# Cross-attention scores with two heads on two row halves of the array, in a six-block Perceiver kernel

## The reference

```python
qh = (q @ Wq + bq).reshape(B, LQ, 16, 16)      # LQ = 256, B = 4
kh = (k @ Wk + bk).reshape(B, 4096, 16, 16)    # k = v = ctx_512
vh = (v @ Wv + bv).reshape(B, 4096, 16, 16)
attn = softmax(einsum('bhqd,bhkd->bhqk', qh, kh) / 4)
out = einsum('bhqk,bhkd->bhqd', attn, vh) @ Wo + bo
```

## Time and profile before

| what | us |
|---|---|
| median of 3 runs | 1431.14 |
| lowest and highest | 1427.41, 1432.78 |
| span of the profiled execution | 1429.1 |
| TensorE busy in it | 1375.6 |
| VectorE busy | 1055.1 |
| ScalarE busy | 922.1 |
| GpSimd busy | 287.6 |

### The profile page before, as it was taken

The page is one execution under the profiler, slowest core; times in us unless marked ns, Lnnn a source line. Parts: engine busy times, 40 slices in busy tenths (PEclk is TensorE's granted clock), DMA queues, the critical chain, the costliest instruction groups (busy, mean ns, idle before and its releaser), DMA issues.

```text
span 1429.1 us, 28070 instructions
## 1 busy us (share of the span) xinstructions
PE 1375.6 (96%) x11138; PEld 846.7 (59%) x11138; DVE 1055.1 (74%) x2114; ACT 922.1 (65%) x1899; POOL 287.6 (20%) x321
## 2 busy tenths in 40 slices
PE   7799999999999999999999999999999999989998
PEld 5355555555555545555554556556557999856666
DVE  4787777787777778777778888835876778767757
ACT  5366777767777767777767666672796664448731
POOL 3354222222222222122213100000003100001210
PEclk9899999999999999999999999999999999999999
DMA  6966555346554545655454743002402320347000
GB/s 184 163 145 143 119 118 111 77 102 130 116 127 92 102 84 125 128 115 113 81 97 101 184 73 61 2 1 60 119 18 65 112 67 1 91 112 155 2 1 30
DMA packets 95587, 133.19 MB, mean 93 GB/s; under 512 B 8864, under 2 KB 70944, under 8 KB 89504
## 3 DMA queue, kind: packets, MB, share of 16 engines
q1 hardware_dynamic: 95456, 131.40, 42.3%
HBM read 94.15 MB, written 37.22 MB: 92 GB/s over the span
## 4 chain that ended last, share of the span: by engine, by line
PE 79%; ACT 8%; DVE 8%; DMA 2%; issue 2%; SPq 1%; POOL 0%; DVEq 0%; ACTq 0%
PE psum L559 16%; PE psum L540 13%; PE psum L524 13%; ACT probs L783 4%; PE psum L2132 4%; PE psum L587 3%; PE psum L2106 3%; DVE peaks L685 3%; PE psum L626 3%; PE psum L1226 2%; PE psum L2851 2%; PE psum L1623 1%; PE psum L275 1%; PE psum L2861 1%; PE psum L2814 1%
## 5 line engine op out<-in xcount | busy, mean ns | idle before, releaser
L685 DVE TENSOR_REDUCE peaks<-psum 128x1 f32<-128x512 f32 x1024 | 643.3, 684 | 197.0 <-PE psum L524 196.4
L783 ACT ACTIVATE probs<-psum 128x512 f32<-128x512 f32 x1024 | 529.0, 615 | 83.3 <-PE psum L540 79.4
L524 PE MATMUL psum<-keysT,queriesT 96*128 96x512 bf16 x1024 | 390.1, 384 | 13.2 <-DMA keysT<-key_parts 7.9
L540 PE MATMUL psum<-queriesT,keysT 98*128 98x256 bf16 x2048 | 392.4, 274 | 6.1 <-ACT queriesT L846 2.4
L540 PEld LDWEIGHTS psum<-queriesT,keysT 98*128 98x128 bf16 x2048 | 176.3, 99 | 191.7 <-ACT probs L783 72.1
L559 PE MATMUL psum<-probs,values 128*17 128x256 f32 x4096 | 245.9, 380 | 0.0
L559 PEld LDWEIGHTS psum<-probs,values 128*17 128x17 f32 x4096 | 107.2, 97 | 102.6 <-issue 27.1
L524 PEld LDWEIGHTS psum<-keysT,queriesT 96*128 96x128 bf16 x1024 | 98.6, 96 | 90.9 <-issue 56.1
L918 POOL CAST key_parts<-key_f 128x512 bf16<-128x512 f32 x57 | 34.8, 611 | 518.0 <-ACT key_f L816 511.0
L816 ACT ACTIVATE key_f<-psum,bk 128x512 f32<-128x512 f32 x59 | 40.5, 687 | 120.7 <-PE psum L587 120.6
L587 PE MATMUL psum<-ctxT,wk 128*128 128x512 f32 x128 | 69.5, 625 | 2.4 <-DVE probs L728 0.9
(11 more groups left out here) (315 smaller groups left out, 1662.5 us busy)
## 6 DMA issues: line engine op xcount, KB each, us to landing
keysT<-key_parts SPq DMA_DIRECT2D x31, 768.0 KB, 7.7
key_parts<-key_parts SPq DMA_DIRECT2D x90, 256.0 KB
keysT<-key_parts SPq DMA_DIRECT2D x31, 512.0 KB, 10.1
ctx_nat<-in_ctx_dram SPq DMA_DIRECT2D x32, 256.0 KB, 3.0
keysT<-key_parts SPq DMA_DIRECT2D x31, 256.0 KB, 11.6
ctx_in<-in_ctx_dram SPq DMA_DIRECT2D x24, 256.0 KB, 5.9
ctx_turned<-ctxT SPq DMA_DIRECT2D x24, 256.0 KB, 4.4
ctx_T<-ctx_turned SPq DMA_DIRECT2D x12, 512.0 KB, 3.8
```

What stands on the lines that cost most here:

```text
L524: e.matmul(ps, self.queriesT[0:ROWS, u % 2, g * GH + j, t * P:(t + 1) * P], self.keysT[0:ROWS, i % RING, j, c * BANK:(c + 1) * BANK], star ...
L540: made = e.matmul(ps[:, j * S:(j + 1) * S], self.keysT[0:AUG, i % RING, j, kt * P:(kt + 1) * P], self.queriesT[0:AUG, u % 2, g * GH + j, : ...
L685: e.tensor_reduce(self.peaks[:, i % 2, pair, c:c + 1], k.ps(("max", n)), AX.X, ALU.max).then_inc(*self.peaked.up(n))
L783: e.activation(self.probs[:, t % RINGP, e2 * GH * S:(e2 + 1) * GH * S], k.ps(("scores", t, e2)), ACT.Exp).then_inc(*self.exped.up((t, e2)))
```

## The change

Head j now has partitions 64 j to 64 j + 63. keysT and queriesT get two planes: MAIN with four of the six part products (64 rows of each head) and REST with the other two and the two maximum rows (34 rows). A score is the sum of two matmuls, MAIN and REST. The maximum uses MAIN alone, 64 rows where it had 96. In a slot the PE issues eight score matmuls of 256 columns, in the order e2, plane, head; then both maxima (one of each head, one after the other), then the weighing, then jobs. A score bank now holds both e2 of one head, so both banks of a slot are signalled by the slot's last two matmuls. Fill keys, turn ctx, turn shift, normalize and make values of later batches move to the next slot with t % 4 == 1 (beside). The result of turn shift is kept by two ACT instructions for one; reading keys and query rows takes four DMAs for three, writing queries five for three. The stream jobs keep their slots.

```diff
+        def beside(slot, job, *numbers):
+            at(slot + (1 - slot) % BLOCK, job, *numbers)
...
-                slot = UNIT * u - 101 + 8 * c
+                slot = UNIT * u - 105 + 8 * c
...
-                    at(slot, "turn ctx", b, c)
+                    beside(slot, "turn ctx", b, c)
...
-                at(slot + 2, "fill keys", u, c)
+                beside(slot + 6, "fill keys", u, c)
...
-            at(SLOTS * i - 2, "turn shift", i)
+            beside(SLOTS * i - 3, "turn shift", i)
...
-                at(SLOTS * i + SLOTS + 4, "normalize", i)
+                beside(SLOTS * i + SLOTS + 4, "normalize", i)
...
-                at(SLOTS * NG * b - 97 + 6 * p, "make values", b, p)
+                beside(SLOTS * NG * b - 97 + 6 * p, "make values", b, p)
...
-            e.matmul(ps, self.queriesT[0:ROWS, u % 2, g * GH + j, t * P:(t + 1) * P],
-                     self.keysT[0:ROWS, i % RING, j, c * BANK:(c + 1) * BANK],
-                     start=True, stop=True).then_inc(*self.max_made.up(n))
+            e.matmul(ps, self.queriesT[own, MAIN, u % 2, g, qt * P:(qt + 1) * P],
+                     self.keysT[own, MAIN, i % RING, c * BANK:(c + 1) * BANK],
+                     start=True, stop=True).then_inc(*self.max_made[j].up(n))
...
-            for e2 in range(2):
-                if 0 <= t < TOTAL:
-                    kt, n = 2 * p + e2, (2 * t + e2) % HALVES
-                    ps = banks.use(n, w, ("scores", t, e2), (self.exped, (t, e2)))
-                    for j in range(GH):
-                        made = e.matmul(ps[:, j * S:(j + 1) * S], self.keysT[0:AUG, i % RING, j, kt * P:(kt + 1) * P],
-                                        self.queriesT[0:AUG, u % 2, g * GH + j, :], start=True, stop=True)
-                    made.then_inc(*self.scored.up((t, e2)))
-                if maxima and not e2:
-                    find_max(maxima[0], t)
+                ps = {}
+                for e2 in range(2):
+                    kt = 2 * p + e2
+                    for plane, rows in ((MAIN, HALF), (REST, TALL)):
+                        for j in range(GH):
+                            if j not in ps:
+                                ps[j] = banks.use(SCORES[(2 * t + j) % len(SCORES)], w, ("scores", t, j), (self.exped, (t, j)))
+                            own = slice(j * HALF, j * HALF + rows)
+                            made = e.matmul(ps[j][:, e2 * S:(e2 + 1) * S], self.keysT[own, plane, i % RING, kt * P:(kt + 1) * P],
+                                            self.queriesT[own, plane, u % 2, g, :], start=(plane == MAIN), stop=(plane == REST))
+                            if e2 and plane == REST:
+                                made.then_inc(*self.scored[j].up((t, j)))
+            for n in maxima:
+                find_max(n, t)
...
-            for n in maxima[1:]:
-                find_max(n, t)
...
-                for e2 in range(2):
-                    w.wait_ge(self.scored, (t, e2))
-                    e.activation(self.probs[:, t % RINGP, e2 * GH * S:(e2 + 1) * GH * S], k.ps(("scores", t, e2)),
-                                 ACT.Exp).then_inc(*self.exped.up((t, e2)))
+                for j in range(GH):
+                    w.wait_ge(self.scored[j], (t, j))
+                    e.activation(self.probs[:, t % RINGP, 2 * j * S:(2 * j + 2) * S], k.ps(("scores", t, j)),
+                                 ACT.Exp).then_inc(*self.exped.up((t, j)))
```

More of the change, by code:

```diff
@@ L297 @@
 RUNS = ((0, 3), (3, 2), (5, 1))
-PAIRS = 6
-ROWS = PAIRS * DH
-AUG = ROWS + 2
+KEY_AT = (1, 2, 0)
+QUERY_AT = ((2, 3), (0, 1), (4,))
+HALF = P // 2
+MAIN, REST = 0, 1
+LOW = 2 * DH
+TALL = LOW + 2
 NG = H // GH
@@ L310 @@
 RINGP = 6
-HALVES, SUMS = 3, 3
+SCORES, SUMS, BLOCK = (0, 1, 2), 3, 4
 MAXES = GH * QT * CH
@@ L512, in find_max @@
         def find_max(n, now):
-            i, r = divmod(n, MAXES)
-            pair, c = self.max_at(n)
-            j, t = divmod(pair, QT)
+            i, j, qt, c = self.max_at(n)
             u, g = divmod(i, UNIT_GROUPS)
+            own = slice(j * HALF, (j + 1) * HALF)
             job, let_go = ("max", n), (self.peaked, n)
@@ L637, in max_at @@
         i, r = divmod(n, MAXES)
-        return divmod(r, CH) if i else divmod(r, GH * QT)[::-1]
+        step, j = divmod(r, GH)
+        qt, c = divmod(step, CH) if i else divmod(step, QT)[::-1]
+        return i, j, qt, c
     def gather(self, e, w, ps, i):
@@ L845, in scalar @@
                     w.wait_ge(self.shiftT_made, i)
-                    e.activation(self.queriesT[ROWS:AUG, u % 2, g * GH:(g + 1) * GH, :].rearrange("p h n -> p (h n)"),
-                                 k.ps(("shiftT", i)).bitcast(BF16)[ROWS:AUG, 0:GH * S], ACT.Copy).then_inc(
-                        *self.shiftT_kept.up(i))
+                    for j in range(GH):
+                        own = slice(j * HALF + LOW, j * HALF + TALL)
+                        e.activation(self.queriesT[own, REST, u % 2, g, :], k.ps(("shiftT", i)).bitcast(BF16)[own, 0:S],
+                                     ACT.Copy).then_inc(*self.shiftT_kept.up(i if j else ("first", i)))
                 elif job == "make values":
@@ L989, in sync @@
                     if i >= RING:
-                        w.wait_ge(self.scored, (SLOTS * (i - RING + 1) - 1, 1))
+                        for j in range(GH):
+                            w.wait_ge(self.scored[j], (SLOTS * (i - RING + 1) - 1, j))
                     self.read_keys(e, i, slice(0, LC), self.keys_here[i % RING], i)
@@ L1002, in sync @@
                     if u >= 2:
-                        w.wait_ge(self.scored, (UNIT * (u - 1) - 1, 1))
-                    for block, run in RUNS:
-                        e.dma_start(self.queriesT[block * DH:(block + run) * DH, u % 2, :, :],
-                                    self.q_dram[b, :, 0:run, :, m, :].rearrange("h i d n -> (i d) h n")).then_inc(
-                            *self.rows_here[u % 2].up(u))
+                        for j in range(GH):
+                            w.wait_ge(self.scored[j], (UNIT * (u - 1) - 1, j))
+                    for plane, rows, parts in ((MAIN, HALF, slice(0, 4)), (REST, LOW, slice(3, 5))):
+                        for j in range(GH):
+                            e.dma_start(self.queriesT[j * HALF:j * HALF + rows, plane, u % 2, :, :],
+                                        self.q_dram[b, j::GH, parts, :, m, :].rearrange("h i d n -> (i d) h n")).then_inc(
+                                *self.rows_here[u % 2].up(u))
                 elif job == "load output weights":
@@ L1017, in read_keys @@
         u, g = divmod(i, UNIT_GROUPS)
-        for block, run in RUNS:
-            e.dma_start(self.keysT[block * DH:(block + run) * DH, i % RING, :, keys],
-                        self.key_dram[u, g * GH:(g + 1) * GH, PARTS - run:PARTS, :, keys].rearrange(
-                            "j i d n -> (i d) j n")).then_inc(*landed.up(key))
+        source = self.key_dram[u, g * GH:(g + 1) * GH, :, :, keys].rearrange("j i d n -> j (i d) n")
+        n = keys.stop - keys.start
+        for j in range(GH):
+            e.dma_start(self.keysT[j * HALF:(j + 1) * HALF, MAIN, i % RING, keys],
+                        source[j, DH:DH + LOW, :].unsqueeze(0).to_broadcast([2, LOW, n])).then_inc(*landed.up(key))
+        for j in range(GH):
+            e.dma_start(self.keysT[j * HALF:j * HALF + LOW, REST, i % RING, keys], source[j, 0:LOW, :]).then_inc(*landed.up(key))
 class Later:
```

60 lines of the change are left out of this document (32 added, 28 removed).

## The result

The changed kernel takes **1854.92 us** (median of 4 runs, 1847.04 to 1873.25) against 1431.62 before: ratio 1.298, 95% interval 1.291 to 1.306. Forecast were 1521 us and a range up to 1595: the sign was right, the size was wrong by a factor of nearly five (+423 for +90).

The account below looks back on a forecast made before the run. PE was taken to set the pace, with ACT close behind. Execution 1429.1 plus 80 us over 102 blocks and 10 in the last 26 gave 1519, forecast as 1521 us, 6% slower; range 1455 to 1595.

Parts of the forecast that it names:

- the one on DMAs: Key and row readings, query writings: bytes unchanged, largest key reading lands in 7.7 us, hidden; nothing, between -4 and +2 us.
- The clock: Rival: PE, busy 80% of a block, falls to 0.90 of its clock; +70 us, 1591; chance 0.05.
- The scores' round trip: Head 1's scores wait for the bank of the previous slot's head 0: 1.20 us a slot, job-free block 6.32 against 5.49.
- the change of tiling: Switching PE between 64-row and other matmuls: 0.10 us; also 0.10 per block with jobs, ends nothing and 0.31.
- The sum without the fault: Whole kernel: 1429.1 + 80 + 10 = 1519 us, forecast as 1521 against the median; chance 0.61.
- the stream jobs: Last 26 blocks: these jobs partly fit into PE's waits of about 0.4 a slot; +10 us, ends 0 and +22.
- Turn shift: Moved behind the weighing, ACT's two copies delay the first exponential by some 0.3 us; block with keys and shift 8.0.
- Jobs: Moved jobs keep their own PE work: keys 0.86 us, values 0.87, shift 0.31, normalize 0.47.
- Trip partly hidden: Rival: shorter latencies, ACT never idle, 0.98 us a slot, job-free block 5.88; 1462 us; chance 0.15.
- no overlap: Rival: row halves don't overlap, trip 1.53 us, block 7.86; 1725 us; chance 0.06.
- Faster, DVE sets the pace: Rival: bank wait over when PE arrives (trip under 0.85 us), maximum banks bind, job-free block 5.5; 1416 us; chance 0.08.

Follow-up runs that it names:

- the mended kernel: The changed kernel with a head's two MAIN key copies read by two 32-row DMAs instead of one repeated-source DMA; 1542.77 us, ratio 1.079.
- run 1: The changed kernel with six key DMAs a group instead of four, none repeating its source; 1542.77 us, ratio 1.079; the same kernel as the mended kernel.
- kernel 1: Another name for the mended kernel, the changed kernel with its key reading cut into separate DMAs; 1542.77 us, ratio 1.079.
- run 3: The kernel before with only the jobs moved to slots that weigh, scores, maxima and reads untouched; 1432.85 us, ratio 1.002.
- run 4: The mended kernel with all jobs back in their slots of the kernel before; 1511.01 us, ratio 1.056.
- run 5: The mended kernel with four score banks and three banks for maxima and jobs; 1510.27 us, ratio 1.055.
- the kernel of 8: The mended kernel with four score banks, weighing every second slot, weighing slots' maxima after it, other job-free slots' maxima after the next slot's scores; 1427.04 us, ratio 0.997.
- the first variant of 8: The kernel of 8 with jobs ahead of the maxima behind the weighing; with normalize or stream jobs, maxima go before the weighing; 1440.82 us, ratio 1.008.

## Why the prediction was right and where it was wrong

**The step that failed** is the one on DMAs: "the bytes of a reading stay. The largest key reading lands 7.7 us after its issue ... hidden". It took a transfer's time from its bytes, while the edit changed how it is cut. It also took the time of one DMA of three: the last of a group's three lands 11.2 us after its own issue (518.13), so the whole reading took 12 us in the kernel before. In the changed kernel it takes 32, more than the 11 slots it has. The same paragraph names what comes late if the cover goes, the first maximum of a group, and that is where PE stood for 242.8 us; but the bound it set, -4 to +2 us, held only as long as the landing time did. No row showed a repeated source, so it should have had a far end of its own, such as the whole of one reading on few engines. Of the 29 us before the first weighing 26 are the same fault in the pieces of group 0: the mended kernel first weighs at 77.7.

**The clock**, a rival at 0.05 with 0.90 and +70 us, came as 0.88, but mostly not for the reason given: the long stops at the keys lowered it. In the mended kernel PE is busy 85% of the stretch from 107 to 1000 us (forecast 80% of a block) and gets 0.98. Yet the rival isn't empty there. Seven times between the first weighing and the last the clock falls to its lower level, for 31 us together, which it never does in that stretch of the kernel before. The windows of run 1 show two blocks with keys and shift, 8.34 us long at 1.00 and 8.97 at 0.88. Blocks in which the clock was low are 0.4 to 1.8 us longer than others with the same jobs, 12 us together, and the sum had nothing for it. All seven falls begin in a block with keys and shift, but five of twelve such blocks, and all twelve that have values too, keep the full clock, so what sets off a fall is open.

**The scores' round trip** was right. On the mended kernel, where it can be read alone, it is 1.20 us a slot (1.20 forecast), a block without jobs 6.32 (6.32), and the halves overlap fully. Its terms hold too: from 730.33 four steps of scores (0.44), the maxima (0.22) and the change of tiling (0.10) make 731.09, the start of the weighing.

**The sum without the fault** was 1521, and kernel 1 takes 1543. From first to last weighing it needs 1005 us where the kernel before needs 893: +112 for +90, of which +97 for +80 lie in the 102 blocks before the stream jobs and +14 for +10 in the rest. The falls of the clock are 12 of the 22 us. Turn shift was undersized: a block with keys and shift is 8.34 us at the full clock, not 8.0, since ACT's two copies last 0.78 and its first exponential comes 1.41 us after the first score instead of 1.1; over the 24 blocks with keys and shift that is some 8 (an estimate). The few us left were not taken apart.

**Jobs.** The claim that a moved job keeps its price was right before (run 3) and wrong after (run 4): with a wait of 0.36 in each slot, moving costs some 30 us. The prediction had counted that effect for the stream jobs alone.

**The rivals.** "Trip partly hidden" and "no overlap" fall by the rows above. "Faster, DVE sets the pace" was priced at 1416 if the trip were gone. Its condition was not met by the change, and with the trip gone in run 5 the maxima's banks, three by then, held the kernel at 1510. That the kernel of 8 takes 1427 is no support for its price: its four slots without jobs take 4.96 us, where the rival had 5.5.

## What to carry to other kernels

Price a DMA that an edit rewrites by its new access pattern, not by its bytes: how the rows are cut decided between 9 and 32 us for the same keys. And take the landing of the last DMA that a consumer waits for, not of the largest. Before pairing work to save engine time, follow each bank from its last reader to its next writer: a saving of 0.88 us a block was bought with three trips of 1.20. Where one engine's phase starves the others, the number of buffers between them must cover its length; moving jobs together or apart only changes how often it doesn't. And when a variant lands in the forecast range, look in its trace whether the reason is the forecast one: in the first variant of 8 it was not.

## What was not expected of the hardware

Two matmuls on 64-row halves overlap completely: after two of 512 columns the next matmul starts 0.22 us on, as after one. A change of tiling, from or to the 64-row matmuls, cost 0.10 to 0.11 us where it could be read. A stop of PE of 7 us was followed by a weighing of 3.58 us for 1.92; over the whole kernel 243 us of such stops came with some 70 us of slower work. And a reading of 1.5 MB of keys took 32 us with two packets under way at a time, 9 us when its DMAs were cut otherwise.
